# Attention weights' maxima moved out of the opening, and one cast moved from ScalarE to VectorE

## The reference, cut to what matters

```python
x = x + 0.5 * ffn(layernorm(x), w_gate, w_up, w_down)
x = x + attn(layernorm(x), norm_w, Wq, Wk, Wv, Wo, gate, log_temperature)
x = x + 0.5 * ffn(layernorm(x), w_gate, w_up, w_down)

def ffn(x, w_gate, w_up, w_down):        # int32 weights in -127..127
    gate = x @ (w_gate / 127).T          # [rows, 384]
    up   = x @ (w_up / 127).T
    return (silu(gate) * up) @ (w_down / 127).T

def attn(x, norm_w, Wq, Wk, Wv, Wo, gate, log_temperature):
    h = rmsnorm(x) * norm_w              # 4 query heads, 2 key/value heads of 32
    q, k, v = l2norm(h @ Wq), l2norm(h @ Wk), h @ Wv
    p = softmax(causal(q @ k.T * exp(log_temperature)))
    return x + gate * ((p @ v) @ Wo)
```

## Time and profile before

| what | value |
|---|---|
| median of 3 runs | 428.96 us (428.58 to 429.21) |
| the profiled execution | 429.13 us, its span in the trace 427.3 us |
| TensorE, share of the span busy | 92% (394.0 us) |
| ScalarE | 87% (371.0 us) |
| VectorE | 82% (348.8 us) |
| GpSimd | 68% (288.5 us) |

### The profile page before, as it was taken

One profiled execution on the slowest core, in us unless ns is written; L12 is line 12 of the kernel. 1 busy time (PEld: TensorE's weight loads), 2 busy tenths in 40 slices (PEclk: granted clock), 3 DMA queues, 4 the chain that ended last, 5 costly groups with the idle time before them and its releaser, 6 DMA issues.

```text
span 427.3 us, 13356 instructions
## 1 busy us (share of the span) xinstructions
PE 394.0 (92%) x5403; PEld 221.6 (52%) x5403; DVE 348.8 (82%) x903; ACT 371.0 (87%) x497; POOL 288.5 (68%) x365
## 2 busy tenths in 40 slices
PE   0689999898999799999999999999999999999995
PEld 0346666674454445535545546446454336676655
DVE  5889999689799978988988988957769938888565
ACT  4799999776898689899898998999988989999961
POOL 5679999986624956767768658662223558999951
PEclk9999999999999999999999999999999999999999
DMA  6487523513714417418347047046123115556452
GB/s 172 102 195 156 69 49 51 100 27 74 126 28 100 75 20 95 88 30 109 66 65 120 17 77 125 3 92 110 38 42 75 27 36 80 109 122 108 117 123 81
DMA packets 119298, 35.25 MB, mean 82 GB/s; under 512 B 101697, under 2 KB 119233, under 8 KB 119233
## 3 DMA queue, kind: packets, MB, share of 16 engines
q1 hardware_dynamic: 117952, 34.02, 43.3%
q10 hardware_dynamic: 1280, 0.33, 0.3%
HBM read 4.98 MB, written 4.19 MB: 21 GB/s over the span
## 4 chain that ended last, share of the span: by engine, by line
PE 59%; DVE 9%; ACT 9%; DMA 7%; POOL 7%; issue 5%; SPq 1%; ACTq 0%; DVEq 0%
PE ps L754 11%; PE ps L519 11%; PE ps L784 11%; PE ps L791 10%; PE ps L583 4%; PE ps L572 4%; DMA QKT<-ST 4%; PE ps L818 4%; ACT XN L471 3%; PE ps L608 3%; ACT PT L898 2%; PE ps L761 2%; DVE H L340 2%; POOL HL L446 2%; ACT SG L489 2%
## 5 line engine op out<-in xcount | busy, mean ns | idle before, releaser
L898 ACT ACTIVATE PT<-ps,k_exp 128x1024 f32<-128x1024 f32 x144 | 153.6, 1117 | 14.4 <-PE ps L761 7.9
L519 PE MATMUL ps<-XT,WT 128*128 128x512 f16 x384 | 94.0, 383 | 5.8 <-DVE H L340 1.9
L754 PE MATMUL ps<-QKT 128*32 128x512 f16 (+1 forms) x1280 | 86.7, 361 | 5.6 <-DMA QKT<-ST 4.5
L791 PE MATMUL ps<-PT,ones 128*32 128x512 f32 (+3 forms) x768 | 76.7, 488 | 0.0
L784 PE MATMUL ps<-PT,V 128*32 128x512 f32 (+3 forms) x768 | 76.3, 487 | 0.0
L446 POOL TENSOR_TENSOR HL<-H,HH 128x1024 f16<-128x1024 f32 x31 | 66.5, 2145 | 8.4 <-ACT HH L495 5.4
L340 DVE SCALAR_TENSOR_TENSOR H<-SG,k_isilu,ps 128x1536 f32<-128x1536 f32 x31 | 56.1, 1809 | 11.2 <-ACT SG L489 5.8
L519 PEld LDWEIGHTS ps<-XT,WT 128*128 128x128 f16 x384 | 34.4, 98 | 50.3 <-issue 10.1
L471 ACT ACTIVATE XN<-X,NB,RS 128x128 f32<-128x128 f32 x128 | 52.5, 483 | 2.4 <-POOL NB L418 2.4
L754 PEld LDWEIGHTS ps<-QKT 128*32 128x32 f16 x1280 | 31.9, 97 | 41.3 <-issue 22.6
L489 ACT ACTIVATE SG<-ps,k_silu 128x1536 f32<-128x1536 f32 x32 | 48.8, 1525 | 4.4 <-DVE H L340 4.3
(11 more groups left out here) (146 smaller groups left out, 671.2 us busy)
## 6 DMA issues: line engine op xcount, KB each, us to landing
result<-X SPq DMA_DIRECT2D x15, 256.0 KB, 2.5
X<-in_L_attn_x SPq DMA_DIRECT2D x7, 512.0 KB, 4.6
X<-in_L_attn_x SPq DMA_DIRECT2D x2, 256.0 KB, 4.7
XT<-w_int SPq DMA_TRANSPOSE x32, 3.1
QKT<-ST SPq DMA_TRANSPOSE x20, 5.5
AXT<-AS SPq DMA_TRANSPOSE x16, 2.8
w_int<-in_L_ffn_w_gate SPq DMA_DIRECT2D x1, 192.0 KB, 3.9
w_int<-in_L_ffn_w_up SPq DMA_DIRECT2D x1, 192.0 KB, 4.4
```

What stands on the lines that cost most here:

```text
L519: i = e.matmul(out[:, j, :], WT[:, wp, w * NJ + j, :], XT[k % 2][:, xp, :], start=a == 0, stop=a == len(passes) - 1)
L754: i_ = e.matmul(dst[r, :].rearrange("p (s a n) -> p s a n", a=2, n=P), QKT[k % 2][:, i // TPC, NH + hp, key0 + r.start:key0 + r.stop], q.r ...
L791: i_ = e.matmul(sums_of(h, 1, n), ones32[:, :], weights_of(g, h, o, n), start=i == 0, stop=i >= TPC * qc, skip_group_check=True)
L898: e.activation(dst, SCORES[(SLOT0[g] + i) % 2][:, :, :], ACT.Exp, scale=k_exp[:, 0:1]).then_inc(a_exp, 1)
```

## The change

Six edits, all in the opening and in FFN 0:

1. The first chain of maxima and powers carries only the two FFN numbers (`m_ffn`). VectorE no longer waits for the attention weights there.
2. The attention weights have their own chain, spread over rounds 1 to 3 of VectorE: `attention_maxima` in round 1, `attention_powers` in round 2, the copy to `pw` and `ipw` in round 3. TensorE's two small products for it stand behind the up products of rounds 1 and 2 and write to a PSUM bank that is free by then.
3. `weights_scaled` moves from round 2 to round 7, behind the last step of the row factors.
4. Statistics are split: those of chunk 1 stand ahead of the power chain and their second half behind it, chunk 3's stand behind the constants `k_silu`, `k_isilu`, `k_ffn`, and chunk 1's low half (x_lo) stands between the two halves of chunk 3's.
5. H of chunk 0 stands ahead of the low weight copies (parts 3 and 4), and its HH is made on VectorE right behind it (`early_h_hi`), no longer on ScalarE.
6. ScalarE's first float16 copy of a normalised chunk waits for the first integer cast alone (`s_cast` 1 in place of 2).

```diff
@@ VectorE, opening
             highest(0, w_flt[:, 0:2 * NJ, :].rearrange("p a b -> p (a b)"))
-            e.wait_ge(s_wo_in, 5 * 16)
-            link(e.tensor_scalar(qkvo[:, 0:NQKV], qkvo[:, 0:NQKV], normw[:, 0:1], None, ALU.mult))
-            highest(2, qkvo[:, 0:NQKV])
-            highest(3, qkvo[:, NQKV:])
             e.wait_ge(s_w[2], 16)
...
-            ffn_dve(e, 0, [("moments", 1)])
+            ffn_dve(e, 0, [("stats", 1)])
             e.wait_ge(s_wpe, 1)
...
+            power_above(m_ffn, bank[0][0:2, 0, 0:P]).then_inc(s_wprep, 1)
+            ffn_dve(e, 0, [("aggregate", 1)])
...
-            ffn_dve(e, 0, [("moments", 2), ("moments", 3)])
+            ffn_dve(e, 0, [("moments", 2)])
             k_values()
-            ffn_dve(e, 0, [("x_lo", 1)])
+            ffn_dve(e, 0, [("stats", 3), ("x_lo", 1), ("aggregate", 3)])
...
             def low_parts_and_hidden():
+                e.wait_ge(s_wready, 1)
+                ffn_dve(e, 0, [("hidden", 0), ("h_hi", 0)])
                 low_parts(3, 4)
-                e.wait_ge(s_wready, 1)
-                ffn_dve(e, 0, [("hidden", 0)])
+
+            def attention_maxima():
+                e.wait_ge(s_wo_in, 5 * 16)
+                link(e.tensor_scalar(qkvo[:, 0:NQKV], qkvo[:, 0:NQKV], normw[:, 0:1], None, ALU.mult))
+                highest(2, qkvo[:, 0:NQKV])
+                highest(3, qkvo[:, NQKV:]).then_inc(s_qmax, 1)
+
+            def attention_powers():
+                e.wait_ge(s_qpe, 1)
+                power_above(m_att, XP[0:2, 0:P]).then_inc(s_qscale, 1)
+
+            def powers_and_rows():
+                e.wait_ge(s_qpe, 2)
+                powers_out(2, XP[:, 2 * P:2 * P + 2])
+                rows("stats", 0)()
+
+            def factors_and_scaled():
+                rows("factors", 3)()
+                weights_scaled()
...
-                    {2: weights_scaled, 3: rows("stats", 0), 4: rows("stats", 1), 5: seed_and_factors,
-                     6: factors_and_weights, 7: rows("factors", 3),
+                    {1: attention_maxima, 2: attention_powers, 3: powers_and_rows, 4: rows("stats", 1),
+                     5: seed_and_factors, 6: factors_and_weights, 7: factors_and_scaled,
@@ ScalarE
-            e.wait_ge(s_cast, 2)
+            e.wait_ge(s_cast, 1)
             ffn_act(e, 0, [("x_hi", 0)])
...
             def h_hi(k, c):
-                if ph and k in (0, NC - 2):
+                if k == 0 or ph and k == NC - 2:
                     return
@@ TensorE
+                e.matmul(XP[0:2, 0:P], colmax[:, 2:4], ident32[:, :], is_transpose=True,
+                         start=True, stop=True).then_inc(s_qpe, 1)
...
+                e.matmul(XP[:, 2 * P:2 * P + 2], m_att[:, 3:4].to_broadcast([2, P]), ident32[0:2, 0:2],
+                         start=True, stop=True).then_inc(s_qpe, 1)
```

More of the change, by code:

```diff
@@ L77, in macaron_kernel @@
         colmax = sb("colmax", [P, 5])
-        m4 = sb("m4", [4, 4])
+        m_ffn, m_att = [sb(n, [2, 4]) for n in ("m_ffn", "m_att")]
         pw = sb("pw", [P, 4])
@@ L165, in macaron_kernel @@
         s_low, s_wtl = sem("s_low"), sem("s_wtl")
+        s_qmax, s_qscale, s_qpe = sem("s_qmax"), sem("s_qscale"), sem("s_qpe")
         (s_cast, s_wo_in, s_one, s_wready, s_wprep, s_wt, s_wpe, s_kact, s_const, s_hot) = [sem("s_" + n) for n in (
@@ L361, in amid, with early_h_hi @@
                     between[k]()
-            def last_h_hi(k, c):
-                if ph and k in (0, NC - 2):
+            def early_h_hi(k, c):
+                if k == 0 or ph and k == NC - 2:
                     e.wait_ge(s_h, c + NC * ph + 1)
@@ L398, in ffn_dve @@
                      for op in (stats, aggregate)]
-            early += [(hidden, 0)]
-            pipeline(e, [(0, hidden), (0, last_h_hi), (0, amid), (6, stats), (0, last_wo_out), (-1, residual), (6, aggregate), (0, last_h_lo)],
+            early += [(hidden, 0)] + [(early_h_hi, 0)] * (1 - ph)
+            pipeline(e, [(0, hidden), (0, early_h_hi), (0, amid), (6, stats), (0, last_wo_out), (-1, residual), (6, aggregate), (0, last_h_lo)],
                      early, after)
@@ L1508, in _, with power_above, powers_out @@
             e.tensor_tensor(colmax[:, 4:5], colmax[:, 0:1], colmax[:, 1:2], ALU.max).then_inc(s_wprep, 1)
-            ffn_dve(e, 0, [("moments", 1)])
-            e.wait_ge(s_wpe, 1)
[L1511 to L1516, removed]
+            ffn_dve(e, 0, [("stats", 1)])
+            def power_above(m, src):
+                link(e.tensor_reduce(m[:, 0:1], src, AXX, ALU.max))
+                link(e.tensor_scalar(m[:, 1:2], m[:, 0:1], 1e-30, None, ALU.max))
+                link(e.tensor_scalar(m[:, 2:3].bitcast(i32), m[:, 1:2].bitcast(i32), 0x7f800000, None,
+                                     ALU.bitwise_and))
+                return e.tensor_scalar(m[:, 3:4], m[:, 2:3], 2.0, None, ALU.mult)
+            def powers_out(lo, src):
+                link(e.tensor_copy(pw[:, lo:lo + 2], src))
+                link(e.tensor_scalar(ipw[:, lo:lo + 2].bitcast(i32), pw[:, lo:lo + 2].bitcast(i32), -1.0,
+                                     float(0x7f000000), ALU.mult, ALU.add))
+            e.wait_ge(s_wpe, 1)
+            power_above(m_ffn, bank[0][0:2, 0, 0:P]).then_inc(s_wprep, 1)
+            ffn_dve(e, 0, [("aggregate", 1)])
             link(e.tensor_reduce(lo1[:, :], bank[0][0:1, 1, 0:P], AXX, ALU.max))
@@ L1519, in _ @@
             e.wait_ge(s_wpe, 2)
-            link(e.tensor_copy(pw[:, :], bank[1][:, 0, 0:4]))
-            link(e.tensor_scalar(ipw[:, :].bitcast(i32), pw[:, :].bitcast(i32), -1.0,
-                                 float(0x7f000000), ALU.mult, ALU.add))
+            powers_out(0, bank[1][:, 0, 0:2])
             def k_values():
@@ L1615, in _ @@
             e.wait_ge(s_wprep, 1)
-            e.matmul(bank[0][0:4, 0, 0:P], colmax[:, 0:4], ident32[:, :], is_transpose=True,
+            e.matmul(bank[0][0:2, 0, 0:P], colmax[:, 0:2], ident32[:, :], is_transpose=True,
                      start=True, stop=True)
@@ L1640, in _, with turn_maxima, spread_powers @@
             hot = is_hot(e)
+            def turn_maxima():
+                e.wait_ge(s_wtl, 3)
+                e.wait_ge(s_qmax, 1)
+                e.matmul(XP[0:2, 0:P], colmax[:, 2:4], ident32[:, :], is_transpose=True,
+                         start=True, stop=True).then_inc(s_qpe, 1)
+            def spread_powers():
+                e.wait_ge(s_qscale, 1)
+                e.matmul(XP[:, 2 * P:2 * P + 2], m_att[:, 3:4].to_broadcast([2, P]), ident32[0:2, 0:2],
+                         start=True, stop=True).then_inc(s_qpe, 1)
             def first_projection(*part):
```

6 lines of the change are left out of this document (3 added, 3 removed).

## The result

The changed kernel took 431.95 us (median of four runs, 431.38 to 432.45), the kernel before 428.78 beside it: ratio 1.0086, 95% interval 1.0064 to 1.0109. I had forecast 431.0, slower by 2.0 us. The direction was right. 431.95 lies within the range of 428.3 to 432.0 by a hair, but the ratio, put on the 428.96 of before, gives 432.65, above it. The profiled execution took 431.61, its span 429.8: 2.5 us over before's 427.3.

A forecast was written before the change was run, and what follows sets the result against it. No engine has room in a 4.6 us FFN 0 round; -1.3 for the lead, +3.67 for round 7, less 0.2, give +2.15, taken as +2.0: 431.0 us, likeliest 430.4 to 431.5, 8 in 10 428.3 to 432.0.

The forecast's parts named there:

- Round 7: Scaling and cast of the attention weights wait for GpSimd's two long instructions, adding 3.67 us to VectorE's round.
- The lead into round 4: Opening and rounds 1 to 3 get shorter, so H(4) starts at 39.9 instead of 41.20, 1.3 us earlier.
- H(0): Instruction making H of chunk 0 in the opening; starts at 19.9 instead of 21.93, 2.0 us earlier.
- between H(0) and H(1): Opening on VectorE: 4.31 us plus 0.62 for the cast HH(0) and 0.70 for low copies; H(1) at 25.5.
- between H(1) and H(4): Rounds 1 to 3 on VectorE: 13.8 us of work plus waits make 14.4 us in place of 14.96.
- the wait of ipw: Round 3: the inverse of two elements waits behind GpSimd's HL(2), taken as 0.3 us; by the skill's pages 0.65.
- H(3)'s wait of 0.31 us for silu(3): Rounds 1 to 3: VectorE still waits for silu of chunk 3 and a residual, about 0.3 us.
- The sum: Whole kernel: -1.3 + 3.67, less 0.2, gives +2.15 us, taken as +2.0 after small losses through attention.
- A: Round 7's scaling meets no long GpSimd instruction and costs 1.05 us; sum -0.45, 428.5 us; chance 0.13.
- B: Kernel gets faster: scaling costs 1.05 us and the lead into round 4 is 2.2; 427.7 us; chance 0.10.
- C: Half a collision in round 7: scaling costs 1.6 to 3.1 us; 429.8 us in the middle; chance 0.17.
- D: Smaller lead: HH(0) waits for GpSimd or w_down comes late, 0.8 us of it; 431.8 us; chance 0.10.

The follow-up runs named there:

- r7_alone: Kernel before with only the three instructions that scale and cast the attention weights moved from round 2 to round 7; 431.32 us, ratio 1.0074.
- psum: Changed kernel with round 7's scaling written to PSUM and the cast and low part reading it there; 428.29 us, ratio 1.0008.
- one_op: Changed kernel with scaling straight to float16, input weights behind H(6) in round 6, output weights last in round 7; 429.69 us, ratio 1.0019.
- fill: psum with four products nobody reads put on TensorE between the first weight transposes and gate(0); ratio 1.0016.
- two_inv: psum with each inverse of two powers written as two instructions of one element; one execution, no time given.
- again: Changed kernel unaltered, run in twelve further executions; median 429.78 us, ratio 1.0035.
- before_shift: Kernel before with 32 unused bytes declared, moving AS and AXT to the changed kernel's addresses; ratio 0.9998.
- after_same: Changed kernel with 224 unused bytes behind the two small tiles, so later tiles keep the kernel before's addresses modulo 256; ratio 1.0068.
- after: The changed kernel itself in its first comparison with the kernel before; 431.95 us, ratio 1.0086.
- after_pad: Changed kernel with 32 unused bytes declared ahead of the attention's tiles; ratio 1.0006.
- before_2: Kernel before unaltered, run once more for a second profile; no time given.
- before_all: Kernel before with four unused tiles that put w_int, XT, AS, AXT, ST and QKT at multiples of 256; 426.26 us, ratio 0.9957.
- best_all: Changed kernel with filling products, single-element inverses, fused scaling behind H(6), factor instructions in round 12, HH(0) on ScalarE, six tiles at multiples of 256; 424.54 us, ratio 0.9925.
- best_pad: best_all with 32 unused bytes in place of its unused tiles; ratio 0.9931.

## Why the prediction was right in direction and too low

- **Round 7: right.** The price is 3.25 us, I said 3.67. VectorE stood where I had put it, 0.56 us behind x_lo's start (57.03 and 56.47; I had 57.58 and 57.01). The 0.42 lie in the handing over: HL ended 2.13 us behind x_lo and not 2.40, and the second multiplication 0.09 us behind HL and not 0.27. The Trainium skill, page "SBUF — State Buffer", section "SBUF: two separate sides", has VectorE's two-port instructions and GpSimd's hold one port pair, each for its whole length. r7_alone (second multiplication 2.15 us), psum (0.34 at its place) and one_op (0.28 alone) agree.
- **The lead into round 4: this step failed.** The prediction made it 1.3 us, it was 0.5, in other runs of the same opening 0.15 to 0.5 at silu(7). Of the 0.8 that are missing, 0.44 lie at H(0), 0.14 between H(0) and H(1) (5.77 us, I had 5.63), and 0.2 between H(1) and H(4) (14.58 us, I had 14.4). First, H(0): I let it follow VectorE and silu(0). It waited 0.52 us for up(0), since TensorE idled 1.95 us ahead of gate(0) and up(0) then took 2.19 us (2.31 to 2.77 in the eight other runs of this opening without filling products), 1.60 before. fill shows that the length of up(0) comes with the gap; an earlier H(0) it doesn't show, since silu(0) was late there. And the gap is there because I followed the weights, and never asked when the first chunk of x lands. Second, the wait of ipw: I took 0.3 us above its 0.17 (128x4, at 12.76 before); it was 0.49 above. The two pages of the Trainium skill that I had set against it, "Vector Engine (DVE) Microarchitecture Reference" (section 5.1) and "SBUF — State Buffer", gave the wait to HL's end, and they were right (37.76, HL to 37.73); two_inv shows the border, one element against two. The same wait stands in the opening (0.49 us at 11.33), where I had put it at nothing. H(3)'s wait of 0.31 us for silu(3) was in the sum.
- **The sum.** +2.15 by my terms; with a lead of 0.5 in place of 1.3, and 3.25 for 3.67, it is about +2.5, which the profiled execution shows. So half of the error in the lead was cancelled by the one in the price, which is luck. Between the medians lay 3.2 in the first comparison and 1.35 in again's, to either side of the sum.
- **What else lay between the medians.** I took the two tiles declared in place of one for nothing. They lengthened 16 transfers by 0.4 to 0.5 us each. No run shows that this alone costs time: before_shift makes the same move in the kernel before and took no longer (0.9998, 0.9979 to 1.0018), after_same and after differ by less than their intervals, and both end 2.5 to 2.7 late in the trace. The stretch at half clock, shown in the last section, goes with more: with it in both kernels, again took 3.4 us more than before (432.04 in two executions, and 428.66), without it in either 1.8 (429.66 and 427.85). All four runs of the changed kernel in the first comparison had it. Why it adds more to the changed kernel stays open.
- Rivals A and B are excluded by the rows of round 7, C too (both waits were there). D, the smaller lead, was right in size (0.8 of lead, 431.8), though not by its mechanism: HH(0) took 0.69 us, unheld, and w_down's cast (7.75) waited for nothing.

## What to carry to other kernels

Before work is moved, look up what GpSimd runs at the new place, and whether two of VectorE's instructions from SBUF to SBUF stand in a row there: one beside GpSimd's end cost its length (0.28 us), the second of a pair the whole of GpSimd's next instruction (2.15). A chain that gets shorter only helps until its partner is late: follow every input of the first joint instruction. And print the tiles' addresses before and after any edit of declarations; 32 bytes changed nothing in before_shift's time, and took the changed kernel's loss away in after_pad. And compare executions with the same mean clock, since one kernel's medians came out at +3.2 and at +1.35 us.

## What the runs showed of the hardware

- **Transposing transfers and 256 bytes.** From issue to landing, AXT<-AS took 2.8 to 2.9 us with both tiles at multiples of 256 (before, before_2, r7_alone, before_all, best_all, after_same), 3.2 to 3.4 at remainders of 32, 64 and 128. QKT<-ST took 4.7 to 4.8 against 5.5 to 5.8, XT<-w_int 2.7 to 2.8 against 3.1. The Trainium skill, page "DMA: Bandwidth & Descriptors", section "How a descriptor splits into AXI transactions", says that a read has to start from a multiple of 256 bytes, and that the bytes ahead of an unaligned start are fetched too and still cost beats of the transfer. The direction agrees. No run shows how these transfers are cut into descriptors, and none separates source from target.
- **A stretch at half clock goes with the longer of two times of one kernel.** In some executions TensorE is granted 0.50 (1.2 GHz) for about 3.5 us inside the attention. It is busy in most of that stretch, but stood idle just ahead of it, waiting for QKT<-ST: 2.80 us in before, up to 146.63. The kernel before, stretches with the granted clock as third number from the right:

```profile
147.00:148.00 1.00, 1.00 (x25) 0.54 (x17) 0.86 (x5) 0.70 (x1) 1.00 (x2) 0.93 0.00 0
148.00:149.00 1.00, 1.00 (x16) 0.57 (x12) 0.90 (x4) 1.00 (x2) 1.00 (x2) 0.50 0.00 0
```

By the runs' mean clocks (0.993 to 0.996 with it), again had it in 2 of 12 executions, 432.04 us against a median of 429.66 in the others, and before in 15 of the 29 beside them, 428.66 against 427.85. All four first runs of the changed kernel had it, where one comparison gave 1.0086 and the other 1.0035. Half the rate for 3.5 us is 1.75 us at most, by estimate, so again's difference of 2.4 is not this stretch alone. Of the 16 profiles with a wait of 2.75 us or more ahead of that place 11 have the stretch, of the four with 1.93 to 1.98 none has it. after_pad and best_pad had it in none of their 18 executions, before_all in 4 of 12 and best_all in 2 of 6, so a shorter wait alone does not keep it away. What does was not tried.
- **TensorE's rate without a change of the granted clock.** At a granted clock of 1.00, up(0), six products of 128x512, took 2.19 to 2.77 us where the engine had stood idle for 1.27 to 1.96 us ahead of gate(0), 1.60 to 2.06 behind 0.62 to 0.78 us (the old opening), and 1.46 to 1.73 where the filling products stood ahead of gate(0).
